# Latent attention: context after the second query block, then both key blocks, output projection, values last

## The reference

```python
scale = DIM_HEAD ** (-0.5)
qn = layernorm(x, ln_q_g, ln_q_b)
q = qn @ Wq * scale
kv = media @ Wkv
k, v = jnp.split(kv, 2, axis=-1)
...
sim = jnp.einsum('bhid,bhjd->bhij', q, k)
sim = jnp.where(media_mask[:, None, None, :], sim, neg_inf)
attn = jax.nn.softmax(sim, axis=-1)
out = jnp.einsum('bhij,bhjd->bhid', attn, v)
out = out.transpose(0, 2, 1, 3).reshape(x.shape[0], x.shape[1], INNER)
attn_out = out @ Wo
x = x + jnp.tanh(attn_gate) * attn_out
```

## Time and profile before

| | |
|---|---|
| median of 3 runs | 2402.78 us (2399.8 to 2403.66) |
| profiled execution | 2400.51 us, of it span of the instructions 2398.7 us |
| granted TensorE clock, mean | 0.963 |
| busy: PE | 2239.8 us (93%) |
| busy: DVE | 1400.3 us (58%) |
| busy: ACT | 1136.0 us (47%) |
| busy: POOL | 653.3 us (27%) |
| latent attention, main loop | about 969 to 1417 us of the span |

### The profile page before, as it was taken

One profiled execution on the slowest core, in us unless ns is written; L12 is line 12 of the kernel. 1 busy time (PEld: TensorE's weight loads), 2 busy tenths in 40 slices (PEclk: granted clock), 3 DMA queues, 4 the chain that ended last, 5 costly groups with the idle time before them and its releaser, 6 DMA issues.

```text
span 2398.7 us, 63756 instructions
## 1 busy us (share of the span) xinstructions
PE 2239.8 (93%) x24770; PEld 1831.9 (76%) x24771; DVE 1400.3 (58%) x2840; ACT 1136.0 (47%) x2617; POOL 653.3 (27%) x833
## 2 busy tenths in 40 slices
PE   8959999979969997999999979998999979989998
PEld 5638888856649996788888859896888866658998
DVE  6746666647753333666666655545666646774333
ACT  5755545436753332444443444445555436664333
POOL 2552222226632221111121110002222216652222
PEclk9979999989989998999999989998999989998999
DMA  7510000020031113000000010000000011011111
GB/s 229 77 17 16 16 16 16 16 74 27 28 91 58 59 57 129 2 2 2 2 2 2 2 37 1 0 0 19 16 16 16 16 42 54 28 38 49 59 59 42
DMA packets 78787, 85.87 MB, mean 36 GB/s; under 512 B 19939, under 2 KB 69680, under 8 KB 78416
## 3 DMA queue, kind: packets, MB, share of 16 engines
q1 hardware_dynamic: 57280, 43.64, 7.2%
q0 software_dynamic: 8368, 21.15, 2.5%
q10 hardware_dynamic: 12896, 17.64, 2.4%
HBM read 52.35 MB, written 21.40 MB: 31 GB/s over the span
## 4 chain that ended last, share of the span: by engine, by line
PE 85%; DVE 4%; ACT 2%; issue 2%; ACTq 1%; POOL 1%; DMA 0%; POOLq 0%; DVEq 0%; SPq 0%
PE ps_all L2223 3%; PE ps_all L2222 3%; PE ps_all L2221 3%; PE ps_all L1476 3%; PE ps_all L1076 3%; PE ps_all L1448 3%; PE ps_all L1853 3%; PE ps_all L999 3%; PE ps_all L1000 2%; PE ps_all L1001 2%; PE ps_all L1046 2%; PE ps_all L1060 2%; PE ps_all L2246 2%; PE ps_all L2248 2%; PE ps_all L2247 2%; PE ps_all L2231 2%
## 5 line engine op out<-in xcount | busy, mean ns | idle before, releaser
L1241 POOL TENSOR_TENSOR s_kx<-s_qkt,const 128x512 f32<-128x512 f32 x128 | 131.7, 1051 | 438.3 <-ACT s_qkt L1171 438.3
L392 POOL TENSOR_TENSOR a_probs<-a_probs,a_sm 128x1024 f32<-128x1024 f32 x32 | 60.9, 1903 | 376.4 <-DVE a_sm L387 376.4
L1599 POOL TENSOR_TENSOR c_kx<-c_qkt,const 128x512 f32<-128x512 f32 x128 | 130.7, 1038 | 111.9 <-ACT c_qkt L1542 111.6
L2221 PE MATMUL ps_all<-f_wh,f_xh 128*128 x396 | 155.2, 392 | 5.6 <-DVE f_xl L2369 5.6
L1179 ACT ACTIVATE s_pt<-ps_all 128x512 f32<-128x512 f32 x128 | 69.7, 597 | 173.1 <-PE ps_all L1060 173.1
L2222 PE MATMUL ps_all<-f_wh,f_xl 128*128 x396 | 149.3, 377 | 0.0
L2223 PE MATMUL ps_all<-f_wl,f_xh 128*128 x396 | 149.2, 377 | 0.0
L2364 DVE SCALAR_TENSOR_TENSOR f_h<-ps_all,rstd,f_act_g 128x688 f32<-128x688 f32 x66 | 61.7, 934 | 144.8 <-PE ps_all L2223 130.6
L1942 ACT ACTIVATE self_w<-ps_all,a_q_bias 128x256 f32<-128x256 f32 x128 | 53.8, 471 | 188.5 <-PE ps_all L1787 188.5
L2246 PE MATMUL ps_all<-f_dh,f_hh 128*128 x396 | 116.9, 295 | 4.0 <-DVE f_hl L2379 4.0
L2285 ACT ACTIVATE f_act_g<-ps_all,rstd 128x688 f32<-128x688 f32 x66 | 55.2, 837 | 133.3 <-PE ps_all L2223 133.3
(11 more groups left out here) (319 smaller groups left out, 7416.4 us busy)
## 6 DMA issues: line engine op xcount, KB each, us to landing
s_v_swap<-s_v_own SPq DMA_DIRECT2D x128, 68.0 KB, 2.0
f_x_in<-x_sorted SPq DMA_DIRECT2D x66, 128.0 KB, 2.0
x_res<-x_sorted SPq DMA_DIRECT2D x66, 128.0 KB, 2.2
x_sorted<-x_res POOLq DMA_DIRECT2D x1, 4224.0 KB, 17.5
l_rows<-in_x SPq DMA_DIRECT2D x32, 128.0 KB, 3.9
x_res<-in_x SPq DMA_DIRECT2D x32, 128.0 KB, 6.0
x_res<-x_back SPq DMA_DIRECT2D x1, 3584.0 KB, 14.4
l_rows<-in_ctx SPq DMA_DIRECT2D x32, 64.0 KB, 5.6
```

The lines of the kernel that those rows point to most:

```text
L1241: ins = nc.gpsimd.tensor_tensor(kx[:, p % 2, c], qkt[:, p % 2, 2 + c].rearrange("p (b k) -> p b k", b=2).unsqueeze(2) .broadcast_to([P, 2, ...
L1599: ins = nc.gpsimd.tensor_tensor(kx[:, p % 2, b], qkt[:, p % 2, 1, b * S:b * S + S].unsqueeze(1).broadcast_to([P, RH, S]), const[:, C_H8X:C ...
L2221: nc.tensor.matmul(bank, x_high, wh[:, w_at], start=(c == 0), stop=False)
```

## The change

In `latent_attention`, in each step of the loop, TensorE's blocks after the second query block take another order: the context of the previous pair first, then both key blocks, then the output projection, then the values of the next pair and, in odd steps, the transposes of x. Before, one key block stood ahead of the context, and the values and transposes stood ahead of the output projection. In VectorE's stream `out_low` moves ahead of the second `k_copy`, and the residual addition ahead of `v_copy`. ScalarE's and GpSimd's streams stay as they are. No instruction is added or removed.

```diff
--- before.py
+++ after.py
@@ -1899,20 +1899,20 @@
                         if more:
                             pe.wait_ge(v_ok.handle, v_ok.at(p + 1))
                             proj_q(g + 1, 2 * i + 1)
-                            proj_k(g + 1, 2 * i)
                         if has(p - 1):
                             pv(p - 1)
                         if more:
+                            proj_k(g + 1, 2 * i)
                             proj_k(g + 1, 2 * i + 1)
-                        if has(p + 1):
-                            proj_v(p + 1)
-                        if i == 1 and has_group2(g + 2):
-                            xt_(g + 2)
                         if has(p - 1):
                             if p == 1:
                                 pe.wait_ge(wlow_ok.handle,
                                            wlow_ok.at(len(q_splits) + len(k_splits) + len(o_splits)))
                             dense(p - 1)
+                        if has(p + 1):
+                            proj_v(p + 1)
+                        if i == 1 and has_group2(g + 2):
+                            xt_(g + 2)
 
                 @block.scalar
                 def _(act):
@@ -2106,17 +2106,17 @@
                             k_copy(g + 1, 2 * i)
                         if has(p):
                             softmax_sum(dve, sm, probs, p, p % 2)
+                        if has(p - 1):
+                            out_low(p - 1)
                         if more:
                             k_copy(g + 1, 2 * i + 1)
                         if has(p - 1):
-                            out_low(p - 1)
+                            residual(p - 1)
                         if has(p + 1):
                             v_copy(p + 1)
                         if i == 1 and has_group2(g + 2):
                             x_low(g + 2)
                             c_low(g + 2)
-                        if has(p - 1):
-                            residual(p - 1)
                 loaded.base += 144
                 close(1, sel_ok, g_pe, affine_ok)
                 close(len(q_splits) + len(k_splits) + len(o_splits), whigh_ok, wlow_ok)
```

## The result

| | before | changed |
|---|---|---|
| median | 2402.43 us (4 runs, 2399.8 to 2403.66) | 2511.09 us (4 runs, 2509.34 to 2513.06) |
| profiled execution | 2400.51 us, span 2398.7 us | 2509.34 us, span 2507.5 us |
| granted clock, mean | 0.963 | 0.953 |

The ratio is 1.0454, 95% interval 1.0436 to 1.0472. The changed kernel is 108.7 us slower by the medians, 108.8 us by the spans.

What follows compares the result with a forecast made beforehand. TensorE, busy 399.33 of 401.00 us in the steady part, was taken as the bound. 2400.5 us plus 87 (waits) plus 41 (clock falls) gave 2529 us, 2530 us on the median's scale; range 2483 to 2553 us.

Steps and rivals of the forecast that it cites:

- The signs: Expected in the profile after: key copy waiting 2.2 us longer, steps about 17 us, 18 with falls, clock 0.85 to 0.95.
- Context with no wait: On TensorE after the second query block: the context follows at once, 0.21 us after the last query matmul, margin 0.4 us.
- The stall: Before the output projection: TensorE waits for VectorE's low halves of the context, 2.91 us a step, p = 1 to 29.
- x's low half: Before the next query block: TensorE waits 0.2 to 0.3 us for this VectorE copy, 14 times, 4 us.
- The sum without the clock: Whole kernel: added waits of 87.4 us with no loss of clock, 2490 us on the median's scale.
- The clock: TensorE's granted clock falls after the new idle gap before the output projection: 1.4 us for 29 steps, 41 us.
- a fall in nearly every step: TensorE's clock was to fall behind the 2.84 us gap before the output projection, counted for 29 steps.
- The price of a fall: Time lost on TensorE each time its granted clock falls behind the gap: taken as 1.4 us, spread 0.9 to 1.6 us.
- the rival of the longer falls: Two slow-clock stretches lie in many steps of the latent-attention loop: 2550 to 2568 us, chance 0.10.
- the clock holds: Same 2.9 us wait before the output projection, but no fall of TensorE's clock: 2490 us, chance 0.24.
- the stall is smaller: VectorE reaches the sums during the context; about 1.1 us wait a step before the output projection: 2435 us, chance 0.04.
- Faster: Even steps' 0.18 us wait at the output projection ends with no new one: 2.5 us gained, 2400 us, chance 0.02.

Runs made afterwards that it cites:

- filled kernel: Changed kernel plus 20 further matmuls of 128x256 in each of 29 steps, between second key block and output projection: 2485.06 us.
- The last experiment: Changed kernel with low halves first, transposes of x before output projection, ScalarE's high halves before exponentials, x's halves (and c_low) before value copies: 2395.04 us, ratio 0.9979.

## Why the prediction was right, point by point

- **Direction and size.** Forecast 2530 us, measured 2511 us, inside 2483 to 2553 us. Slower was right.
- **The signs.** The key copy waits 3.70 us where it waited 1.49 us, 2.2 us more, as said. The weight loads of the values waited for the key copies 29 times before, 19.0 us in all, and no longer do. Steps at the full clock are 17.37 and 16.50 us long (I had said about 17), those with a fall 17.9 to 20.1 us, but for the shorter last one (I had said 18). The mean clock of 0.95 is at the upper edge of what I gave.
- **Context with no wait.** Right: 1271.03 comes 0.21 us after the last query matmul.
- **The stall, 2.91 us a step, 2.84 us of it idle.** Measured 2.69 us, 29 times. From key block 2i's last matmul to the output projection I had worked out 3.82 us (1157.27 to 1161.09); it is 1277.42 - 1273.74 = 3.68 us. The difference lies in two terms: sums start 0.61 us after the key copy and not 0.68 as in the earlier trace rows, and the low halves take 1.22 us and not 1.28. I had taken both from one step of before; the earlier trace rows, where the low halves follow the reciprocal as they do here, already had 1.22 us.
- **x's low half, 0.2 to 0.3 us in 14 steps.** Right: 3.3 us in 14. That the transposes themselves cost more behind the values was missed: 0.59 us there, where they had taken 0.41 us ahead of the output projection.
- **The sum without the clock, 2490 us on the median's scale.** The filled kernel, which has the waits and no falls, has 2485.06 us. By the steps of the trace the sum of 87.4 us came out as 86 us. That it is so close is in part luck: even steps lose 2.58 us and not 2.73, odd steps 3.23 us and not 3.1 to 3.2, and the errors go against each other.
- **The clock, 41 us.** The mechanism was right and the size was off: 26 us by the medians, 22 us by the steps. The step of the prediction that failed is "a fall in nearly every step": 14 of the 29 gaps had one. The price of a fall was right: I had taken 1.4 us, and 12 of them cost 1.2 to 1.6 us; two cost 2.6 to 2.7 us, as in the rival of the longer falls. The upper bound of 78 us counted 2.7 us for each of 29 gaps; here two gaps cost that, and the kernel with VectorE's old order has ten steps of that kind. The evidence for the count was a single fall behind a gap of 2.03 us; I read it as a limit, and it was a case. Gaps of 2.1 us cost 12 us, of 2.7 us 22 to 26 us, and of 3.3 us some 54 us (26, and the 28 of the kernel with VectorE's old order). The forecast lies 19 us too high, most of it by this term; the range was wide enough to hold it. Which of the gaps bring a fall, no run here tells.
- **The rival "the clock holds"**, 2490 us, is excluded by the mean clock of 0.95 and by the filled kernel. The rule of the Trainium skill, "TensorE: Matmul & The Clock Gate", section "HAM oscillation", by which gaps of this length should leave the clock alone, does not hold for the runs of this kernel; gaps of 1.5 us do leave it alone.
- **The rival "the stall is smaller"** (sums run during the context) is what the kernel with the sums first does, when the program order is changed for it: 2446.69 us against the 2435 us that I had given. In the changed kernel itself the order forbids it.
- **"Faster"** had its deciding point in VectorE's chain being under 0.9 us; it is 3.7 us from the block's last matmul, so the changed kernel could not reach it. The last experiment shows that TensorE's order allows it when the other engines follow. What I had said of that, that little could be won because only 1.67 us of 401 were idle, was wrong: the steady part lost 6.4 us. The busy time counts a matmul to its end (0.28 us) while the next may start after 0.12 us, so a step of 0.21 us into a new block does not show as idle.

## What to carry to other kernels

When a block is moved on a full engine, ask which chain of another engine it was hiding, and add up that chain in the order of its own queue: a copy that waits for the moved block holds everything that is queued behind it, though that work was ready long before. Moving two blocks can take cover from both ends of one chain: here moving the context ahead of a key block cost 1.5% alone, moving the output projection ahead of the values 1% (with VectorE's order changed along with it), both 4.5%, and putting the low halves' two instructions ahead of the waiting copy gave nine tenths of it back. Where TensorE is the bound, price a new gap twice, once for the wait and once for the clock, and take the clock's share as a count of falls times the price of one, since the two can be wrong apart; and look for what can be won in the spacing of the starts, not in the idle time alone.

## What the runs showed of the hardware that I had not expected

- Gap and clock do not stand in a yes-or-no relation. With the same work around it, repeated in 29 steps, a gap of 1.5 us left the clock at 1.00 in every step; 2.1 us brought a fall in 8 of the 29 (mean clock 0.97), 2.7 us in 14 (0.95), and 3.3 us in all 29 (0.88).
- The price of one fall hardly depended on the gap: 1.2 to 1.6 us behind gaps of 2.7 us, 1.4 to 1.5 us behind gaps of 2.1 us. The steps with a mean clock of 0.83, which cost about twice as much, were 2 behind gaps of 2.7 us and 10 behind gaps of 3.3 us.
- Idle TensorE time can be dearer than work: 580 useless matmuls in the gaps made the kernel 26 us faster (1%).
- The same copy is followed by the next VectorE instruction after 0.61 us in one order and 0.68 us in another, with the same duration of 0.69 us in the record. No run here settles why.
